# Linear attention and sparse FFN on one core: query products with the running sums as float32 instead of three fp32r passes, query pairs in four buffers, and another order on VectorE

## The chip, the cores and the metric

One core of a Trainium2 chip runs the whole program. The metric is the device time of one execution in microseconds (us). Engines: TensorE (PE; PEld is its weight load), VectorE (DVE), ScalarE (ACT), GpSimd (POOL) and SyncE (SP, which only issues transfers here).

## The reference

Input x has 2 batches x 1024 rows x 512 columns, float32. Weights have the shapes below.

```
xn  = layernorm(x)
q   = xn @ Wq.T   16 heads of 128;   k, v = xn @ Wk.T, xn @ Wv.T   4 heads of 128
q,k = rope(q), rope(k);   qf = elu(q) + 1;   kf = elu(k) + 1
for each row s:  state += kf_s (x) v_s;   z += kf_s
                 out_s = (qf_s . state) / (qf_s . z + 1e-6)
x   = x + layernorm(out @ Wo.T)
h   = silu(xn2 @ Wgate) * (xn2 @ Wup)        xn2 = layernorm(x), 512 -> 2048
h   = the two largest by magnitude of each four kept, the others 0
x   = x + layernorm(h @ Wdown)
```

Four query heads share one key and value head.

## The kernel before, in words

**Number formats.** To keep float32 precision at the fp32r matmul rate most operands are split: hi is the value rounded to fp32r, lo is the value minus hi. A product is then three passes, hi x hi, lo x hi, hi x lo (`three`, lines 453 to 456; `project`, 458 to 463, does it for four contraction blocks, twelve passes). ScalarE writes hi, GpSimd or VectorE writes lo (line 1148 on GpSimd, `split`, `query_low`, `key_low`).

**Units and slots.** The attention has 8 units (batch x key head) of 8 slots; a slot is 128 rows for the four query heads of the unit. The recurrence is done blockwise. For a block, the scores (keys x queries, line 564, bank psS) are masked causally into Sf (line 974). The result is Sf times the values (line 542), plus the queries times the running sums of the blocks before (lines 545 to 547), not in a unit's first slot. The values have two more columns, ones and zeros, so that a product of 130 columns also gives the denominator. The running sums (key rows x value rows) are accumulated in bank psSt over the unit (line 552). ScalarE copies them to Sth (line 776), VectorE takes the low half Stl (line 968). Then VectorE forms the quotient (lines 980, 983, 986) into Tn; four transposes (line 585) bring it to psS; Ah (ScalarE, line 792) and Al (VectorE, line 1006) are its halves, and one slot later the output product with Oh and Ol (line 578) is added into Y (line 1002).

**The order.** It is written out by hand for each engine: `slot_a(s)` for 65 + 1 ticks of the attention, `slot_f(n)` for the FFN, in one list TICKS (line 36). In slot s TensorE does: the products and sums of block m = s - 1; every fourth slot the transposes of the values; the scores of block s; the output product of block s - 2; the transposes of the quotient of block s - 1; every fourth slot the transposes of the keys; one query projection, `queries(s + 7)`; in some slots also the projection of keys or values (`k_slot`, `v_slot`, lines 54 to 59) and the transposes of normalised input rows (`turn`, slots IN_1, MID_0).

**Queries** come in pairs of heads (j = i // 2), one pair every two slots. For a pair VectorE rotates (`rotate`, lines 917 to 921, and `rotate_sum`, line 926). The projection of queries is laid out so that the two halves of a head stand on different banks; four transfers (`pair_rows`, lines 394 to 402, issued on SP's queue) bring them back to whole heads in the buffer xq. ScalarE takes Exp and Relu (lines 743, 744), VectorE adds them (`query_sum`, line 931), ScalarE writes the hi half (line 750), GpSimd the lo half (line 1183). The scores of block group p wait for pool_fl, which counts those lo halves. There is one buffer xq for all pairs but pair 1.

**Keys** of group p: `swap_keys` (ScalarE), `rotate_keys` (VectorE, lines 939, 940, 944), `key_terms` (ScalarE), `key_sum` (VectorE, line 948), `key_split` (ScalarE), `key_low` (GpSimd).

**Weights** come through a ring of four staging buffers. PLAN (lines 112 to 134) gives each piece the tick in which its halves are made; SP issues the load of piece k + 4 in the tick in which piece k is split, and waits for that split.

In its odd slots VectorE does rotate and rotate_sum of a pair, in its even slots query_sum and, in slots 4p - 2, rotate_keys; then the low half of the sums, the mask, the quotient, key_sum, the addition to Y, Al, output weight splits and statistics.

Of the kernel before, what the change touches and what calls it, by code (L numbers as in the profile page):

```python
# [13 lines left out]
P = 128  # L14
# [39 lines left out]
def k_slot(p):  # L54
    return 4 * p - 3 if p > 1 else -1


def v_slot(p):
    return 4 * p - 2 if p > 1 else 0
# [8 lines left out]
IN_1 = [3, 4, 7, 8, 11, 12, 15, 16]  # L68
MID_0 = [39, 40, 43, 44, 47, 48, 51, 52]
# [42 lines left out]
def weight_plan():  # L112
    plan = [(("k", 0, 0), -1), (("q", 0, 0), -1), (("q", 0, 1), -1), (("q", 0, 2), -1), (("v", 0, 0), -1),
            (("q", 0, 3), -1)] + [(("o", 0, h), -1) for h in range(4)]
    for u in range(1, UNITS + 1):
        base = 8 * (u - 1)
        more = u < UNITS
        if more:
            plan += [(("q", u, 0), (base - 2) if u > 1 else -1), (("q", u, 1), (base - 1) if u > 1 else -1), (("q", u, 2), base)]
        else:  # L120
            plan += [(("g", 0, 0), base - 1), (("g", 0, 1), base)]
        if u > 1:
            plan += [(("o", u - 1, h), base + 1) for h in range(4)]
        if more:
            plan += [(("q", u, 3), base + 2), (("k", u, 0), base + 3), (("v", u, 0), base + 4)]
# [41 lines left out]
def build(nc, x, wq, wk, wv, wo, wg, wu, wd, cos_t, sin_t, causal, eye, x1, out):  # L167
    with ExitStack() as ctx:
# [7 lines left out]
        with ExitStack() as early:  # L176
            KTr = early.enter_context(nc.sbuf_tensor("kt_rows", [P, 4, P], F32))
            Vr = early.enter_context(nc.sbuf_tensor("v_rows", [P, 4, VP], F32))
        D0h, D2h = sb("d_hi0", [P, W], F32R), sb("d_hi2", [P, VP * 4], F32R)
        Xh = sb("x_hi", [P, 4, KT, W], F32R)  # L180
# [11 lines left out]
        Dk = sb("d_lo0", [P, W], F32R)  # L192
        Dv = sb("d_lo2", [P, W], F32R)
        Uh = sb("u_hi", [P, W], F32R)
        Ul = sb("u_lo", [P, W], F32R)
        Ah = sb("a_hi", [P, 4, P], F32R)
        Al = sb("a_lo", [P, 4, P], F32R)
        Sth = sb("st_hi", [P, VP], F32R)
        Stl = sb("st_lo", [P, VP], F32R)
# [3 lines left out]
        scr = sb("scratch", [P, 16, W])  # L203
# [14 lines left out]
        M1, M2, xq = scr[:, 0:2, :], scr[:, 2:4, :], scr[:, 4:6, :]  # L218
        E = M2
        cosb = scr[:, 6:8, :]  # L220
        sinb = scr[:, 8:10, :]
        rotk, xk, Ek, Sf, zero, Tn = [scr[:, i, :] for i in range(10, 16)]
# [3 lines left out]
        def pair_of(j):  # L226
            if j == 1:
                return psOD, Y[:, 0:2, :], Y[:, 2:4, :], scr[:, 13:15, :]
            return psQ, M1, M2, xq
# [10 lines left out]
        hid = scr[:, 0:4, :]  # L240
        ab = scr[:, 4:8, :]
        sg = scr[:, 8, :]
        Wmax = [scr[:, 9, :], ab[:, 1, :]]
        msk = scr[:, 10:13, :].rearrange("p a t -> p (a t)").bitcast(BF16).rearrange("p (a t) -> p a t", a=6)
# [64 lines left out]
        act_sth, act_ah = sem("act_sth"), sem("act_ah")  # L309
        dve_q, dve_x, dve_f = sem("dve_q"), sem("dve_x"), sem("dve_f")  # L310
        dve_k1, dve_k2, dve_kx, dve_kf = sem("dve_k1"), sem("dve_k2"), sem("dve_kx"), sem("dve_kf")
        dve_stl, dve_s = sem("dve_stl"), sem("dve_s")
# [40 lines left out]
        def _(sp):  # L353
# [937 lines left out]
```

## Time and profile before

| what | value |
|---|---|
| time of the runs, median of 3 | 1279.67 us (1279.66 to 1280.18) |
| profiled execution, own time | 1280.5 us |
| its span | 1278.4 us |
| mean granted TensorE clock | 0.99 |
| TensorE, VectorE, GpSimd, ScalarE busy | 96%, 63%, 39%, 38% |
| attention slots 1 to 64 in the span | about 61 to 739 us, the FFN behind it |

How to read it: the span is from the first to the last instruction of the profiled execution; 2.1 us lie around it. A matmul's printed duration is modelled and includes the way through the array, so consecutive matmuls overlap; the distance between two starts tells what one costs. "idle before" is time without any work in flight on the engine, and behind the arrow stands what ended it. The granted clock is a share of 2.4 GHz: 1.00 is 2.4 GHz, 0.50 is 1.2 GHz.

### The profile page before, as it was taken

The page shows a single profiled execution, that of the slowest core. Times are in us where ns is not written, and L with a number is a line of the kernel's source. Part 1 is how long each engine was busy: PE and PEld are TensorE (multiplying, and loading weights), DVE is VectorE, ACT ScalarE, POOL GpSimd, SP SyncE. Part 2 cuts the span into 40 slices and gives each one's busy share as a digit, 9 for nine tenths or more (in the row PEclk, how much of TensorE's full clock was granted, in tenths as well). Part 3 has the DMA queues.
Part 4 walks back from the last instruction along what each step waited for, and adds up shares of the span by engine and source line. Part 5 has one row for each costly group of instructions (what it writes and reads, how often), then busy time and mean ns, then how long its engine had stood idle before and what let it go on. Part 6 is the DMA issues. An engine that isn't in the chain of part 4 may idle for free.

```text
span 1278.4 us, 16486 instructions
## 1 busy us (share of the span) xinstructions
PE 1232.3 (96%) x6271; PEld 1037.8 (81%) x6271; DVE 807.9 (63%) x1354; ACT 484.6 (38%) x802; POOL 498.8 (39%) x444
## 2 busy tenths in 40 slices
PE   8889999999999999999998999999999999999996
PEld 7678888788788887887886887888888878888884
DVE  8666666655766666667565655666656755555568
ACT  4433444433444434344434333333333333333322
POOL 6333342323254523334223444344435653333414
PEclk9899999999999999999998999999999999999998
DMA  5421322221323323212212321221213321111103
GB/s 185 107 67 54 86 58 51 68 57 37 96 83 107 91 58 83 62 46 84 50 34 75 107 91 58 67 67 58 58 50 99 98 75 50 43 57 42 50 1 115
DMA packets 50350, 90.33 MB, mean 71 GB/s; under 512 B 6496, under 2 KB 6752, under 8 KB 50272
## 3 DMA queue, kind: packets, MB, share of 16 engines
q1 hardware_dynamic: 50272, 89.29, 24.7%
q8 instruction: 50, 0.82, 0.3%
q14 instruction: 28, 0.23, 0.1%
HBM read 64.09 MB, written 8.39 MB: 57 GB/s over the span
## 4 chain that ended last, share of the span: by engine, by line
PE 81%; DVE 12%; ACT 2%; issue 2%; DMA 2%; SPq 1%; POOL 1%; DVEq 0%
PE bank_q L456 8%; PE bank_q L454 8%; PE bank_q L455 8%; PE bank_od L454 4%; PE bank_od L455 4%; PE bank_od L456 4%; PE bank_t L454 4%; PE bank_t L455 4%; PE bank_t L456 4%; PE bank_od L542 4%; PE bank_y L454 4%; PE bank_y L456 4%; PE bank_y L455 4%; PE bank_s L456 3%; PE bank_s L455 3%; PE bank_s L454 3%
## 5 line engine op out<-in xcount | busy, mean ns | idle before, releaser
L1148 POOL TENSOR_TENSOR big_lo<-scratch,big_hi 128x1024 fp32r<-128x1024 f32 (+1 forms) x64 | 152.2, 2388 | 346.5 <-ACT big_hi L824 214.1
L1148 POOL TENSOR_TENSOR w_lo<-stage,w_hi 128x512 fp32r<-128x512 f32 x96 | 137.1, 1436 | 148.0 <-ACT w_hi L708 147.1
L454 PE MATMUL bank_q<-x_hi,w_hi 128*128 128x512 f32 x440 | 177.7, 404 | 0.0
L456 PE MATMUL bank_q<-x_lo,w_hi 128*128 128x512 f32 x440 | 172.7, 392 | 0.0
L455 PE MATMUL bank_q<-x_hi,w_lo 128*128 128x512 f32 x440 | 171.9, 391 | 0.0
L815 ACT ACTIVATE scratch<-scratch 128x512 f32<-128x512 f32 x64 | 40.4, 632 | 207.1 <-DVE scratch L1069 207.1
L1085 DVE TENSOR_TENSOR y_acc<-bank_od,y_acc 128x512 f32<-128x512 f32 x44 | 30.2, 687 | 118.6 <-PE bank_od L456 118.6
L454 PE MATMUL bank_y<-wout_hi,a_hi 128*128 128x512 f32 x256 | 101.6, 397 | 1.6 <-POOL wout_lo L1148 1.2
L792 ACT CAST a_hi<-bank_s 128x512 fp32r<-128x512 f32 x64 | 37.5, 587 | 165.6 <-PE bank_s L585 165.6
L456 PE MATMUL bank_y<-wout_lo,a_hi 128*128 128x512 f32 x256 | 100.3, 392 | 0.0
L455 PE MATMUL bank_y<-wout_hi,a_lo 128*128 128x512 f32 x256 | 99.6, 389 | 0.0
L542 PE MATMUL bank_od<-v_rows,scratch 128*128 128x130 f32 x488 | 98.2, 291 | 0.0
L456 PEld LDWEIGHTS bank_q<-x_lo,w_hi 128*128 128x128 f32 x440 | 83.0, 189 | 18.3
L455 PEld LDWEIGHTS bank_q<-x_hi,w_lo 128*128 128x128 f32 x440 | 83.3, 189 | 15.9
L454 PEld LDWEIGHTS bank_q<-x_hi,w_hi 128*128 128x128 f32 x440 | 83.1, 189 | 15.4
L1148 POOL TENSOR_TENSOR wout_lo<-stage,wout_hi 128x512 fp32r<-128x512 f32 x28 | 44.4, 1600 | 91.4 <-ACT wout_hi L708 91.4
L542 PEld LDWEIGHTS bank_od<-v_rows,scratch 128*128 128x128 f32 x488 | 75.8, 191 | 3.8
L454 PE MATMUL bank_t<-x_hi,w_hi 128*128 128x512 f32 x192 | 77.2, 402 | 0.9 <-ACT kt_rows L728 0.7
L455 PE MATMUL bank_t<-x_hi,w_lo 128*128 128x512 f32 x192 | 76.5, 398 | 0.0
L456 PE MATMUL bank_t<-x_lo,w_hi 128*128 128x512 f32 x192 | 76.2, 397 | 0.0
L824 ACT CAST big_hi<-scratch 128x512 fp32r<-128x512 f32 x64 | 39.2, 622 | 86.5 <-DVE scratch L1041 76.1
L545 PE MATMUL bank_od<-st_hi,big_hi 128*128 128x130 f32 x212 | 65.2, 308 | 0.0
(238 smaller groups left out, 3146.9 us busy)
## 6 DMA issues: line engine op xcount, KB each, us to landing
scratch<-scratch SPq DMA_DIRECT2D x124, 128.0 KB, 2.4
x_rows<-x SPq DMA_DIRECT2D x56, 256.0 KB, 3.0
stage<-wq SPq DMA_DIRECT2D x32, 256.0 KB, 2.7
stage<-wo SPq DMA_DIRECT2D x32, 256.0 KB, 2.6
stage<-wg SPq DMA_DIRECT2D x32, 256.0 KB, 2.7
stage<-wu SPq DMA_DIRECT2D x32, 256.0 KB, 2.8
stage<-wd SPq DMA_DIRECT2D x32, 256.0 KB, 2.7
x<-x_rows SPq DMA_DIRECT2D x16, 256.0 KB, 2.5
```

Of the source, the lines that this page charges most:

```text
L454: pe.matmul(ps, whi, xhi, start=first, stop=False, skip_group_check=True)
L455: pe.matmul(ps, wlo, xhi, start=False, stop=False, skip_group_check=True)
L456: return pe.matmul(ps, whi, xlo, start=False, stop=last, skip_group_check=True)
L542: ins = pe.matmul(o, Sf[:, h * P:(h + 1) * P], Vr[:, c, :], start=True, stop=first, skip_group_check=True)
L545: pe.matmul(o, qh, Sth[:, :], start=False, stop=False, skip_group_check=True)
L792: copy(Ah[:, :, :].rearrange("p h t -> p (h t)"), psS[:, :]).then_inc(act_ah, 1)
L815: act.activation(ab[:, i, :], hid[:, i, :], ACT.Abs).then_inc(act_ab, 1)
L824: copy(big_h[:, d % 2, i, :], hid[:, i, :]).then_inc(act_hh, 1)
L1085: dve.tensor_tensor(Y[:, t, :], down_bank(y), Y[:, t, :], ALU.add).then_inc(dve_yf, 1)
L1148: return pool.tensor_tensor(dst, full, hi.bitcast(F32), ALU.subtract)
```

## The change

It has these parts:

- The product of queries and running sums is one float32 matmul per head, on rows of queries kept in Q and on one float32 copy St of the sums. Sth, Stl and line 968 go; who waited for them waits for ScalarE's copy.
- Whole heads of pairs are kept in four buffers of Q (two groups) instead of one; `pair_rows` waits for the split of three pairs before and for the products that read the buffer last.
- TensorE projects `queries(s + 6)` in slot s, not s + 7. Keys of group p are projected in slot 4p - 4 (before 4p - 3), values in 4p - 3 (before 4p - 2), and keys(1) in slot 0 instead of ahead of it. Rotation of a pair is one slot later (even slots), query_sum too (odd slots); pair_rows(2) moves behind four weight loads on SP's queue.
- On VectorE the quotient stands ahead of the mask, rotate_sum behind the mask, rotate_keys behind that, key_sum behind Al.
- Some rows' transposes and weight splits have other ticks; the scratch tiles are laid out anew (hidden gets a tile of its own, which shares memory with Q).

```diff
 def k_slot(p):
-    return 4 * p - 3 if p > 1 else -1
+    return 4 * p - 4
 def v_slot(p):
-    return 4 * p - 2 if p > 1 else 0
+    return 4 * p - 3
-IN_1 = [3, 4, 7, 8, 11, 12, 15, 16]
-MID_0 = [39, 40, 43, 44, 47, 48, 51, 52]
+IN_1 = [3, 6, 7, 10, 11, 14, 15, 18]
+MID_0 = [39, 42, 43, 46, 47, 50, 51, 54]
 # weight_plan
-            plan += [(("q", u, 0), (base - 2) if u > 1 else -1), (("q", u, 1), (base - 1) if u > 1 else -1), (("q", u, 2), base)]
+            plan += [(("q", u, 0), (base - 1) if u > 1 else -1), (("q", u, 1), base if u > 1 else -1)]
-            plan += [(("q", u, 3), base + 2), (("k", u, 0), base + 3), (("v", u, 0), base + 4)]
+            plan += [(("q", u, 2), base + 2), (("k", u, 0), base + 2), (("v", u, 0), base + 4), (("q", u, 3), base + 4)]
 # sync, pair_rows
-                if j > 1:
-                    g.wait_ge(pool_fl, pair_before(j) + 1)
+                if j > 3:
+                    g.wait_ge(pool_fl, j - 3)
+                    g.wait_ge(pe_pv, 4 * (j // 2 - 1))
-            pair_rows(2)
-                if kind == "a" and i % 2 and i <= 57:
-                    pair_rows((i + 5) // 2)
+                if kind == "a" and i % 2 == 0 and i <= 58:
+                    pair_rows((i + 4) // 2)
 # tensor
                     if not first:
-                        g.wait_ge(dve_stl, 7 * u + ms)
+                        g.wait_ge(act_st, 7 * u + ms)
                         if not first:
-                            pe.matmul(o, qh, Sth[:, :], start=False, stop=False, skip_group_check=True)
-                            pe.matmul(o, qh, Stl[:, :], start=False, stop=False, skip_group_check=True)
-                            ins = pe.matmul(o, ql, Sth[:, :], start=False, stop=True, skip_group_check=True)
+                            ins = pe.matmul(o, Q[:, (2 * p + h // 2) % 4, h % 2, t], St[:, :], start=False, stop=True,
+                                            skip_group_check=True)
-                if s + 7 < SLOTS:
-                    queries(s + 7)
+                if s + 6 < SLOTS:
+                    queries(s + 6)
-            keys(1)
 # scalar
-                        g.wait_ge(pe_pv, m)
+                        g.wait_ge(pe_pv, m + 1)
-                        copy(Sth[:, :], psSt[:, 0:VP]).then_inc(act_sth, 1)
+                        copy(St[:, :], psSt[:, 0:VP]).then_inc(act_st, 1)
-                if s % 2 == 0 and s and s + 4 < 2 * STEPS * 2:
-                    query_split((s + 4) // 2)
+                if s % 2 and s + 3 < 2 * STEPS * 2:
+                    query_split((s + 3) // 2)
-                if s % 2 and s + 5 < 2 * STEPS * 2:
-                    query_terms((s + 5) // 2)
+                if s % 2 == 0 and s + 4 < 2 * STEPS * 2:
+                    query_terms((s + 4) // 2)
 # vector, slot_a: the new order
+                if s % 2 == 0 and s + 4 < 2 * STEPS * 2:
+                    rotate((s + 4) // 2)
+                if s % 2 and s + 3 < 2 * STEPS * 2:
+                    query_sum((s + 3) // 2)
...
+                if 0 <= s < SLOTS:
...
+                if s % 2 == 0 and s + 4 < 2 * STEPS * 2:
+                    rotate_sum((s + 4) // 2)
                 for p in range(1, STEPS):
                     if s == k_slot(p) + 1:
-                        key_sum(p)
+                        rotate_keys(p)
+                if s % 4:
+                    for job in before:
+                        split_x(job)
...
+                for p in range(1, STEPS):
+                    if s == k_slot(p) + 1:
+                        key_sum(p)
 # gpsimd
-                if s % 2 == 0 and s + 4 < 2 * STEPS * 2:
-                    query_low((s + 4) // 2)
+                if s % 2 and s + 3 < 2 * STEPS * 2:
+                    query_low((s + 3) // 2)
```

In the new order of VectorE the quotient of block s - 1 stands behind rotate or query_sum and ahead of the mask of block s.

## Rows read from the trace of the kernel before

**Rows 1.** The page: busy us of each engine, share of the span, instructions.

```profile
PE 1232.3 (96%) x6271; PEld 1037.8 (81%) x6271; DVE 807.9 (63%) x1354; ACT 484.6 (38%) x802; POOL 498.8 (39%) x444
```

**Rows 2.** The page, chain that ended last: shares of the span by engine.

```profile
PE 81%; DVE 12%; ACT 2%; issue 2%; DMA 2%; SPq 1%; POOL 1%; DVEq 0%
```

**Rows 3.** List of waits, TensorE, whole span: us in total, times, longest.

```profile
PE bank_s L585 <- DVE scratch L986: 19.9, 15, 4.3
...
PE bank_y L454 <- POOL wout_lo L1148: 1.2, 1, 1.2
...
PE bank_y L454 <- DVE wout_lo L905: 0.4, 1, 0.4
```

**Rows 4.** Instructions grouped by line, TensorE, 60 to 760 us: count, busy us, mean ns.

```profile
L545 PE MATMUL bank_od<-st_hi,big_hi 128*128 128x130 f32 x212 | 65.2, 308 | 0.0
```

**Rows 5.** Timeline, TensorE, a unit's first products: start us, us, line.

```profile
61.00 1.05 PE L542 MATMUL bank_od<-v_rows,scratch 128*128 128x130 f32 x8
61.90 0.39 PE L552 MATMUL bank_st<-v_rows,kt_rows 128*128 128x130 f32 x2
62.04 0.47 PE L454 MATMUL bank_s<-big_hi,k_hi 128*128 128x512 f32 x1
```

**Rows 6.** Timeline, TensorE in a slot without a wait, and ScalarE's copy.

```profile
429.66 0.38 PE L542 MATMUL bank_od<-v_rows,scratch 128*128 128x130 f32 x2
...
432.03 0.47 PE L454 MATMUL bank_s<-big_hi,k_hi 128*128 128x512 f32 x1
...
432.81 0.40 PE L454 MATMUL bank_y<-wout_hi,a_hi 128*128 128x512 f32 x1
...
435.56 0.60 PE L585 MATMUL bank_s<-ident,scratch 128*128 128x128 f32 x4
...
438.74 0.38 PE L542 MATMUL bank_od<-v_rows,scratch 128*128 128x130 f32 x2
...
432.37 0.27 ACT L776 CAST st_hi<-bank_st 128x130 fp32r<-128x130 f32 x1 [1.93 <-PE bank_st L552]
```

**Rows 7.** Timeline, VectorE, a unit's first odd slot.

```profile
404.38 1.23 DVE L917 TENSOR_TENSOR scratch<-bank_q,scratch 128x1024 f32<-128x1024 f32 x1 [1.07 <-PE bank_q L456]
...
406.84 1.23 DVE L926 TENSOR_TENSOR scratch<-scratch 128x1024 f32<-128x1024 f32 x1
...
409.18 0.69 DVE L986 TENSOR_TENSOR scratch<-bank_od,small 128x512 f32<-128x512 f32 x1
```

**Rows 8.** Timeline, TensorE, the slot behind it: a wait at the transposes.

```profile
421.12 0.39 PE L454 MATMUL bank_y<-wout_hi,a_hi 128*128 128x512 f32 x1
...
423.69 0.66 PE L585 MATMUL bank_s<-ident,scratch 128*128 128x128 f32 x4 [1.73 <-DVE scratch L986]
```

**Rows 9.** Timeline, ScalarE behind the transfers, and VectorE's query_sum beside GpSimd's work.

```profile
412.36 1.06 ACT L743 ACTIVATE scratch<-scratch 128x1024 f32<-128x1024 f32 x1 [0.44 <-DMA scratch<-scratch]
...
330.03 2.30 DVE L931 SCALAR_TENSOR_TENSOR scratch<-scratch 128x1024 f32<-128x1024 f32 x1
```

**Rows 10.** Timeline, GpSimd in that stretch.

```profile
329.91 3.58 POOL L1148 TENSOR_TENSOR wout_lo<-stage,wout_hi 128x512 fp32r<-128x512 f32 x2 [12.13 <-ACT wout_hi L708]
```

**Rows 11.** Timeline, before and in slot 0, TensorE and SP's queue.

```profile
48.40 0.50 PE L454 MATMUL bank_t<-x_hi,w_hi 128*128 128x512 f32 x1 [0.68 <-ACT kt_rows L728]
...
52.04 0.47 PE L454 MATMUL bank_s<-big_hi,k_hi 128*128 128x512 f32 x1 [0.62 <-POOL big_lo L1148]
...
55.69 1.07 SPq L363 DMA_DIRECT2D stage<-wq  x2
```

**Rows 12.** Three stretches: us, busy time of each engine, then PEclk, DMA share, GB/s.

```profile
68.30:71.70 3.40, 3.40 (x10) 2.65 (x9) 1.48 (x3) 0.56 (x2) 1.00 (x3) 0.50 0.85 245
404.00:440.00 36.00, 33.25 (x186) 28.16 (x184) 25.26 (x39) 15.44 (x25) 17.71 (x16) 1.00 0.37 103
686.20:692.80 6.60, 5.25 (x15) 4.29 (x16) 3.90 (x9) 2.71 (x5) 4.67 (x5) 0.50 0.19 49
```

**Rows 13.** Timeline, TensorE, slot 58.

```profile
687.55 0.69 PE L585 MATMUL bank_s<-ident,scratch 128*128 128x128 f32 x2 [2.19 <-DVE scratch L986]
```

More of the change, by code:

```diff
@@ L216, in build @@
         den, share = small[:, 44:48], small[:, 48:52]
-        M1, M2, xq = scr[:, 0:2, :], scr[:, 2:4, :], scr[:, 4:6, :]
+        M1, M2 = scr[:, 0:2, :], scr[:, 2:4, :]
         E = M2
-        cosb = scr[:, 6:8, :]
-        sinb = scr[:, 8:10, :]
-        rotk, xk, Ek, Sf, zero, Tn = [scr[:, i, :] for i in range(10, 16)]
+        cosb = scr[:, 4:6, :]
+        sinb = scr[:, 6:8, :]
+        rotk, xk, Ek, Sf, Tn = [scr[:, i, :] for i in range(8, 13)]
         vT = rotk
@@ L227, in pair_of @@
             if j == 1:
-                return psOD, Y[:, 0:2, :], Y[:, 2:4, :], scr[:, 13:15, :]
-            return psQ, M1, M2, xq
+                return psOD, Y[:, 0:2, :], Y[:, 2:4, :], Q[:, 1, :, :]
+            return psQ, M1, M2, Q[:, j % 4, :, :]
         def pair_landed(gate, j):
@@ L238, in pair_before @@
             return 0 if j == 2 else j - 1
[L240 to L244, printed above, removed]
+        ab = scr[:, 0:4, :]
+        sg = scr[:, 4, :]
+        Wmax = [scr[:, 5, :], ab[:, 1, :]]
+        msk = scr[:, 6:9, :].rearrange("p a t -> p (a t)").bitcast(BF16).rearrange("p (a t) -> p a t", a=6)
         c01, c23, pw, qw, rr, m2 = [msk[:, i, :] for i in range(6)]
@@ L953, in slot_a @@
                 before = at(tick - 1, lambda j: turn_tick(*j), [j for j in TURNS if j in LATER])
-                if s % 2 and s + 5 < 2 * STEPS * 2:
-                    rotate((s + 5) // 2)
-                    rotate_sum((s + 5) // 2)
-                if s % 2 == 0 and s and s + 4 < 2 * STEPS * 2:
-                    query_sum((s + 4) // 2)
-                for p in range(1, STEPS):
-                    if s == k_slot(p) + 1:
-                        rotate_keys(p)
-                if s % 4:
-                    for job in before:
-                        split_x(job)
-                if 0 <= m < SLOTS and m % 8 < 7:
-                    i = m // 8 * 7 + m % 8
-                    g.wait_ge(act_sth, i + 1)
-                    dve.tensor_tensor(Stl[:, :], psSt[:, 0:VP], Sth[:, :].bitcast(F32),
-                                      ALU.subtract).then_inc(dve_stl, 1)
-                if 0 <= s < SLOTS:
-                    g.wait_ge(mask_ld, 16)
-                    g.wait_ge(pe_s, s + 1)
-                    g.wait_ge(pe_pv, s)
-                    dve.tensor_tensor(Sf.rearrange("p (h t) -> p h t", h=4),
-                                      psS[:, :].rearrange("p (h t) -> p h t", h=4),
-                                      mask[:, :].rearrange("p (o t) -> p o t", o=1).to_broadcast([P, 4, P]),
-                                      ALU.mult).then_inc(dve_s, 1)
+                if s % 2 == 0 and s + 4 < 2 * STEPS * 2:
+                    rotate((s + 4) // 2)
+                if s % 2 and s + 3 < 2 * STEPS * 2:
+                    query_sum((s + 3) // 2)
                 if 0 <= m < SLOTS:
@@ L988, in slot_a @@
                                       ALU.mult).then_inc(dve_a, 1)
+                if 0 <= s < SLOTS:
+                    g.wait_ge(mask_ld, 16)
+                    g.wait_ge(pe_s, s + 1)
+                    g.wait_ge(pe_pv, s)
+                    dve.tensor_tensor(Sf.rearrange("p (h t) -> p h t", h=4),
+                                      psS[:, :].rearrange("p (h t) -> p h t", h=4),
+                                      mask[:, :].rearrange("p (o t) -> p o t", o=1).to_broadcast([P, 4, P]),
+                                      ALU.mult).then_inc(dve_s, 1)
+                if s % 2 == 0 and s + 4 < 2 * STEPS * 2:
+                    rotate_sum((s + 4) // 2)
                 for p in range(1, STEPS):
                     if s == k_slot(p) + 1:
-                        key_sum(p)
+                        rotate_keys(p)
+                if s % 4:
+                    for job in before:
+                        split_x(job)
                 if 0 <= m2 < SLOTS:
@@ L1011, in slot_a @@
                         split_x(job)
-                if s == 0:
-                    query_sum(2)
                 for k in pieces_at(tick, "o"):
@@ L1134, in _ @@
             query_sum(1)
-            rotate(2)
-            rotate_sum(2)
             for kind, i in TICKS:
```

33 lines of the change are left out of this document (13 added, 20 removed).

## The prediction

> **What bounds the kernel now.** I began with the page's busy shares [rows 1]: TensorE is busy 96% of the span and VectorE 63%. The page's chain of waits gives TensorE 81% of what ended last and VectorE 12% [rows 2]. So time is won by shortening TensorE's own stream, or by removing its waits. The list of waits [rows 3] says how much the waits are: 19.9 us in 15 for line 986, the quotient on VectorE that the four transposes of line 585 read, and 1.2 + 0.4 us for output weights. Everything else there is small. All of these lie between 61 and 731 us, in the attention's 65 slots.
>
> The profiled execution took 1280.5 us (span 1278.4), the median of the runs shown is 1279.67. I add my terms to 1280.5 and take 0.8 us off at the end.
>
> **Part 1: fewer passes in the query products.** Per head, line 542 stays, and lines 545 to 547 (three fp32r products of 130 columns) become one float32 product, in 7 of a unit's 8 slots. That is 56 slots; line 545 has 212 = 4 x 53 records on bank_od [rows 4], and three slots near the end use bank_q. What a float32 product of just this shape costs is shown by the first slot of a unit, where line 542 runs alone: 8 records for 4 products, then 2 records of line 552, and the scores begin at 62.04 after a start at 61.00 [rows 5]. A float32 product is two records, and ten records take 1.03 us. From the first to the ninth record is 0.90 us, 0.112 us each. In an ordinary slot the same stretch goes from 429.66 to 432.03 [rows 6]: 2.37 us for 8 + 12 + 2 = 22 records, also near 0.11 each. After the change it has 8 + 8 + 2 = 18 records: 1.03 + 8 x 0.112 = 1.93 us. That is 0.45 us less in a slot, 56 x 0.45 = **25.0 us less**, all on TensorE's path. Its operands are others than line 542's (query rows as weights, the sums as columns), but type and shape are the same, so I take this row; the ends are 0 (as long as the three passes it replaces) and 27 us (a record at 1.03 / 10 below what I took, in all of them).
>
> The trace shows two records' time for a float32 product. The Trainium skill, in "FP8 and Floating Point Precision", section "TensorE Precision Notes", says that true FP32 makes four passes through the array, which speaks against the swap of three passes for one product. What it would do here is rival D.
>
> **Part 2: work that leaves or moves.** Line 968 (the low half of the sums, 0.28 us on VectorE) goes, and TensorE then needs only ScalarE's copy. The copy began at 432.37, the next slot's products at 438.74 [rows 6], so nothing is gained there but VectorE's time. The new waits of the row transfers (the products' count, and the split of three pairs before) were fulfilled by work of the slot before or of the same slot's beginning: nothing. Memory is laid out anew without another wait in the FFN.
>
> **Part 3: the quotient is earlier.** Before, an odd slot ran rotate, rotate_sum, low half, mask, quotient. In a unit's first odd slot rotation begins at 404.38, and the quotient's last step comes only at 409.18 [rows 7]. In the next slot key rotation and query_sum stood in front of it, and TensorE waited 1.73 us [rows 8]. This pair of waits recurs in each unit: 19.9 less 4.3 (slot 1) and 2.2 (slot 58) is 13.4 us in 13 waits. Behind the printed wait hides a little more: from the last group of line 454 at 421.12 to 423.69 is 2.57 us, where three passes need 0.69 (432.81 to 435.56 is twelve [rows 6]): 1.88 lost for a wait of 1.73; with the slower restart I take 0.2 us each, 13 x 0.2 = 2.6. After the change neither rotate_sum nor the key rotation stands ahead of the quotient. At a unit's first odd slot: query_sum 1.2 (2.3 when GpSimd works beside it [rows 9, 10]), the quotient's three steps 1.0, against transposes due at 1.03 + 0.78 + 2.75 = 4.6 us. I remove all of it: **16.0 us less**.
>
> **Part 4: the pair's round trip is tighter.** Despite its name "quotient first" leaves two things ahead of it: rotate in even slots, query_sum in odd ones. The trip from rotate_sum to query_sum is 4.3 us for four transfers (rotate_sum ends at 408.07, ScalarE begins at 412.36 [rows 7, 9]) and 2.0 us for Exp and Relu, 1.0 each. TensorE's slot becomes 1.93 (products) + 0.78 (scores) + 2.75 (output) + 3.18 (transposes and a projection) = 8.64 us by the starts [rows 6]. An elementwise step of 512 columns holds its engine 0.5 to 0.6 us, one of 1024 twice that [rows 7, 9]. With these, slot 8k+1 of unit k (10.5 us, with values): mask done 3.7 in, key rotation 2.5, then on ScalarE key terms 1.1, pair split 1.0, attention copy 0.5: 8.8; back on VectorE low half, key_sum and two output-weight splits 2.4, and hops of 0.2: 11.4. So VectorE reaches rotate of slot 8k+2 0.9 us late. Then rotate 2.4, quotient 1.0, mask 0.6, rotate_sum 1.3: 6.2; trip 6.3: 12.5, which is 3.9 into the next slot; query_sum 1.2 to 2.3 (GpSimd splits two weights then; beside its work query_sum took 2.30 [rows 9, 10]) and quotient 1.0 make 6.1 to 7.2. The transposes are due at 1.93 + 0.78 + 2.75 = 5.46. So a new wait of 0.6 to 1.7 us, I take 1.2, in seven units: **8.4 us more**, between 0 (VectorE not late) and 17. In the other half of a unit (8k+6, no output weights) rotate starts before TensorE's slot does, query_sum ends 3.8 in, the quotient at 4.9: no wait, 0.6 us to spare. Slots 8k and 8k+4 hold the keys' projection too, so their pairs come back in time. GpSimd finishes the output weights about 1 us before TensorE reads them; what is late next is that split.
>
> **Part 5: the start.** keys(1) is no longer before slot 0. Before, it filled 48.40 to 51.2 of the time in which TensorE waited for GpSimd's low half (the scores start at 52.04 [rows 11]). Now TensorE idles from 47.7 to 52.0, and the granted clock may fall as it did behind the 4.3 us wait (0.50, the 1.2 GHz level, for 3.4 us from 68.3 [rows 12], costing 1.7). pair_rows(2) now stands on SP's queue behind loads that wait for GpSimd's splits (issued at 55.69 [rows 11]), so it starts near 56.3: ScalarE at 60.8, done 62.8, query_sum 64.1, quotient 65.1, after which query(7) and values(1) end at 71.1, 72.8 with the clock. Before, slot 2 began at 72.1 with one projection more (2.8 us) done. **3.5 us more**, between 0 and 7.
>
> **Part 6: the end.** Slot 57 gains query(63) and values(15), so the output weights are ready for slot 58: the waits of 1.2, 0.4 and 2.2 us [rows 3, 13] go, 4.4 with their restarts. But slots 58 and 59 are now about 5.9 us, and pair 31 is rotated in slot 58: rotate_sum ends 5.0 in, trip to 11.4, query_sum and quotient to 13.7, against transposes due at 5.9 + 5.5 = 11.4: a wait of 2.3 (2.5). The clock fell there to 0.50 for 6.6 us, costing 3.3 [rows 12]; with one wait in place of three I count half of it. 4.4 - 2.5 + 1.7 = **3.6 us less**, between 0 and 6.
>
> **The sum.** -25.0 - 16.0 + 8.4 + 3.5 - 3.6 = -32.7; 1280.5 - 32.7 - 0.8 = **1247.0 us**.
>
> **The rivals.**
> A. The new waits of part 4 don't come, because VectorE is not late: -41.1, so 1238.6. For: in the wait of rows 8 VectorE was held by work that moves behind the quotient. Against: the walk above has it over by 0.6 even at its best.
> B. The waits of part 4 are twice as long or bring falls of the clock (1.7 us each in seven units, 12 us): +8 to +12, 1255 to 1259. For: a wait of 4.3 us was followed by one. Against: waits up to 1.7 us were not; the clock was 1.00 from 404 to 440, which holds two of them [rows 12].
> C. **It ends slower: the pair's return becomes the bound.** Place: query_sum in every odd slot, ahead of the quotient. Let the trip be 2.5 us longer than 6.3 (transfers queued behind weight loads on SP, ScalarE held by key_terms). Then 8k+3 waits 3.7, 8k+7 1.9, 8k+1 and 8k+5 about 1.3 together: 6.9 x 7 = 48 in place of 8.4, 1287. It decides against the change from about 2.2 us on. Against: the trip was 4.3 and 2.0 us here, and SP's blocks end before the transfers are due.
> D. The float32 product takes four passes of 0.112 us where three stood: +0.112 x 4 x 56 = +25 in place of -25, 1297. Against: a product of this type and shape took two records of 0.112 [rows 5]. The Trainium skill's page named in part 1 has this rule.
> E. The change does not do what it says: if VectorE held TensorE back in every slot, the saved passes would turn into waits and only parts 3 to 6 count, 1272. Against: 96% on TensorE.
>
> **How the numbers follow.** Forecast 0.50, A 0.18, B 0.20, C 0.05, D 0.02, E 0.05. The range takes in A and B with the bounds of parts 5 and 6 (3.5 us on either side each) and what the walks of parts 4 to 6 miss: 1233 to 1266. C, D and E are outside, 0.12, and a little of A beyond its bounds, 0.06. Faster by over 0.2% are the forecast, A, B, E and a thin end of C; 0.2% (2.6 us) is about what a measurement of this kernel can tell from no change. Faster 0.92, same 0.02, slower 0.06.
>
> **What would show it.** Right: line 546 and 547 gone and one product with two records per head; from the first product to the scores 1.93 us; TensorE's waits for line 986 gone from slots 8k+1 and 8k+2 and standing in 8k+3 at about 1.2 us, one near slot 59; idle of 4 us before slot 0's scores. Wrong: a slot's product stretch above 2.1 us (part 1), waits in 8k+7 or 8k+1 (part 4), waits on output weights, or a granted clock of 0.5 within the units.

## The result and the profile after

The changed kernel takes **1300.18 us** (median of 4 runs, 1296.48 to 1303.86) where the kernel before takes 1279.66 beside it: ratio 1.0163, 95% interval [1.0137, 1.0189]. It is slower by 1.6%. The forecast was 1247.0, within 1233 to 1266, with 0.92 on faster: **wrong in sign**. The profiled execution took 1296.48 us (span 1294.7), 16.0 more than the one of before.

The page of the changed kernel, busy shares, and the chain that ended last (they answer to [rows 1] and [rows 2]):

```profile
PE 1217.1 (94%) x6047; PEld 1022.3 (79%) x6047; DVE 808.6 (62%) x1298; ACT 482.7 (37%) x802; POOL 487.6 (38%) x444
...
PE 69%; DVE 19%; ACT 4%; issue 3%; DMA 2%; SPq 1%; POOL 1%; DVEq 0%; ACTq 0%
```

TensorE has 224 instructions less, as it should (four a slot in 56 slots), yet its share of the chain fell from 81% to 69%; VectorE's rose from 12% to 19%, ScalarE's from 2% to 4%. The time went into waits. The list of TensorE's waits (us in total, times, longest), to set beside [rows 3]:

```profile
PE bank_s L581 <- DVE scratch L963: 26.9, 13, 5.0
PE bank_t L480 <- DVE x_lo L888: 22.8, 6, 4.3
...
PE bank_s L452 <- POOL big_lo L1130: 4.3, 1, 4.3
```

The 19.9 us for the quotient are gone. In their place stand 26.9 us for the mask (line 963: the transposes write the scores' bank, which the mask must have read), and 22.8 us, in only six waits, for x_lo, the low half of transposed rows of x. The prediction does not name that tile. (Both lists also hold one wait of 6.5 us for x_lo on bank_s, before slot 0; it is the same in both kernels.)

**The product is as cheap as forecast.** TensorE's timeline in slot 36, from the first product to the work behind it (it answers to [rows 6]):

```profile
446.01 0.39 PE L539 MATMUL bank_od<-v_rows,scratch 128*128 128x130 f32 x2
446.23 0.39 PE L542 MATMUL bank_od<-st_rows,q_rows 128*128 128x130 f32 x2
...
447.80 0.39 PE L548 MATMUL bank_st<-v_rows,kt_rows 128*128 128x130 f32 x2
448.02 0.60 PE L501 MATMUL bank_t<-ident,scratch 128*128 128x128 f32 x4
```

From 446.01 to 448.02 are 18 records in 2.01 us, 0.112 each, and from the products to the sums' product 1.79 for 16. Slot 11, shown below, goes from its first product at 170.89 to its scores at 172.82: 1.93 us, the forecast. A plain slot (one without a projection of keys or values, a turn of x rows or a wait, such as slot 38), start to start, takes 8.66 us; the forecast was 8.64, and the kernel before had 9.09.

**Where the time came from.** From the first product of slot 1 to that of slot 64 it took 664.8 us before and 681.6 now: +16.8, all of the difference between the profiled executions. Six slots carry more than that: 7, 11, 15, 43, 47 and 51 take 12.60, 16.06, 12.57, 16.05, 12.57 and 16.21 us, 28.8 more than the same six before. Those are the slots 4p - 1 in which x rows are turned (IN_1, MID_0). The timeline of all engines at one of them, slot 11:

```profile
170.46 0.60 PE L480 MATMUL bank_t<-ident,x_rows 128*128 128x128 f32 x4
...
170.89 0.39 PE L539 MATMUL bank_od<-v_rows,scratch 128*128 128x130 f32 x2
...
172.45 1.06 ACT L736 ACTIVATE scratch<-q_rows 128x1024 f32<-128x1024 f32 x1 [3.24 <-DMA q_rows<-scratch]
...
172.82 0.48 PE L452 MATMUL bank_s<-big_hi,k_hi 128*128 128x512 f32 x1
...
173.42 1.04 ACT L737 ACTIVATE q_rows<-q_rows 128x1024 f32<-128x1024 f32 x1
174.37 1.12 ACT L701 CAST w_hi<-stage 128x512 fp32r<-128x512 f32 x2
174.49 1.23 DVE L921 SCALAR_TENSOR_TENSOR q_rows<-scratch,q_rows 128x1024 f32<-128x1024 f32 x1 [5.06 <-ACT q_rows L737]
...
175.39 0.57 ACT L676 CAST x_hi<-bank_t 128x512 fp32r<-128x512 f32 x1
...
176.65 0.68 DVE L963 TENSOR_TENSOR scratch<-bank_s,mask 128x512 f32<-128x512 f32 x1
177.24 0.68 DVE L888 TENSOR_TENSOR x_lo<-bank_t,x_hi 128x512 fp32r<-128x512 f32 x1
...
178.07 0.87 PE L480 MATMUL bank_t<-ident,x_rows 128*128 128x128 f32 x3 [4.31 <-DVE x_lo L888]
```

One row of x is turned at the end of slot 4p - 2, the next in the middle of slot 4p - 1, **ahead of the output product, into the same bank**. Between the two the bank must be read twice. But ScalarE stands idle for 3.24 us in query_terms until the pair lands, then does Exp, Relu and two weight splits before x_hi (175.39); VectorE has query_sum, the quotient and the mask ahead of x_lo (177.24). TensorE stands for 4.31 us, and its output product behind it. Before, the turns were in slots 4p - 1 and 4p (transposes into bank_t at 127.94 in slot 7, 144.08 in slot 8, 171.96 in slot 11), never less than 16 us apart.

The clock follows. Windows of the changed kernel (us, busy time of PE, PEld, DVE, ACT, POOL, then PEclk, DMA share, GB/s), behind the waits of slots 7, 11 and 43:

```profile
130.60:136.00 5.40, 5.40 (x28) 4.54 (x29) 1.68 (x3) 2.64 (x4) 2.82 (x2) 1.00 0.01 3
...
176.60:183.30 6.70, 5.23 (x15) 4.29 (x16) 1.32 (x3) 1.58 (x3) 5.06 (x4) 0.50 0.36 117
...
528.20:534.90 6.70, 5.38 (x15) 4.44 (x16) 1.18 (x2) 1.53 (x2) 4.92 (x4) 0.50 0.34 120
```

Behind slot 7's wait of 3.30 us the clock stayed at 1.00; behind the two of 4.3 it was 0.50, the 1.2 GHz level, for some 6.7 us, and so it was behind slot 51's. That goes with slots 11, 43 and 51 being 3.5 us longer than the other three: 1.0 by the wait, and half of the 5.2 to 5.7 busy us at half clock.

### The profile page after: what moved, and what is told of

It is laid out like the page before. It is cut to its first block, busy times and chain, and to the rows that moved or that the text cites. A ratio compares the mean times of both kernels' runs of the same rounds, so it can differ in the third digit from the quotient of the medians.

```text
span 1294.7 us, 15921 instructions
## 1 busy us (share of the span) xinstructions
PE 1217.1 (94%) x6047; PEld 1022.3 (79%) x6047; DVE 808.6 (62%) x1298; ACT 482.7 (37%) x802; POOL 487.6 (38%) x444
## 4 chain that ended last, share of the span: by engine, by line
PE 69%; DVE 19%; ACT 4%; issue 3%; DMA 2%; SPq 1%; POOL 1%; DVEq 0%; ACTq 0%
PE bank_q L454 7%; PE bank_q L452 7%; PE bank_q L453 7%; PE bank_od L452 4%; PE bank_od L453 4%; PE bank_od L454 4%; PE bank_t L454 3%; PE bank_t L453 3%; PE bank_t L452 3%; PE bank_od L539 3%; PE bank_s L452 3%; PE bank_s L453 3%; PE bank_s L454 3%; PE bank_y L452 3%; PE bank_y L453 3%
## 5 line engine op out<-in xcount | busy, mean ns | idle before, releaser
L1130 POOL TENSOR_TENSOR big_lo<-hidden,big_hi 128x512 fp32r<-128x512 f32 x32 | 73.6, 2320 | 214.5 <-ACT big_hi L814 214.5
L805 ACT ACTIVATE scratch<-hidden 128x512 f32<-128x512 f32 x64 | 40.5, 634 | 206.9 <-DVE hidden L1053 206.9
L921 DVE SCALAR_TENSOR_TENSOR q_rows<-scratch,q_rows 128x1024 f32<-128x1024 f32 x31 | 38.0, 1226 | 126.2 <-ACT q_rows L737 126.2
L1130 POOL TENSOR_TENSOR big_lo<-q_rows,big_hi 128x1024 fp32r<-128x1024 f32 x32 | 76.5, 2392 | 98.8 <-ACT big_hi L743 98.7
L453 PE MATMUL bank_y<-wout_hi,a_lo 128*128 128x512 f32 x256 | 102.4, 400 | 0.0
L539 PE MATMUL bank_od<-v_rows,scratch 128*128 128x130 f32 x488 | 91.2, 276 | 0.0
L542 PE MATMUL bank_od<-st_rows,q_rows 128*128 128x130 f32 x424 | 82.7, 277 | 0.0
```

Of the source, the lines that this page charges most:

```text
L453: pe.matmul(ps, wlo, xhi, start=False, stop=False, skip_group_check=True)
L539: ins = pe.matmul(o, Sf[:, h * P:(h + 1) * P], Vr[:, c, :], start=True, stop=first, skip_group_check=True)
L542: ins = pe.matmul(o, Q[:, (2 * p + h // 2) % 4, h % 2, t], St[:, :], start=False, stop=True, skip_group_check=True)
L805: act.activation(ab[:, i, :], hid[:, i, :], ACT.Abs).then_inc(act_ab, 1)
L921: dve.scalar_tensor_tensor(whole, grown, 1.0, whole, ALU.min, ALU.add).then_inc(dve_f, 1)
L1130: return pool.tensor_tensor(dst, full, hi.bitcast(F32), ALU.subtract)
```

## The experiments

Each run stood beside the kernel before on the same chip; "after" is the changed kernel. Differences between two kernels are of their medians.

**1. The rows of x first.**

```diff
 # scalar: in slot 4p - 2 ahead of query_terms, not behind it in 4p - 1
+                if s % 4 == 2:
+                    for job in at(tick, lambda j: turn_tick(*j), [j for j in TURNS if j in LATER]):
+                        split_x(job)
 # vector: in slot 4p - 1 ahead of query_sum, not behind the mask
+                if s % 4 == 3:
+                    for job in before:
+                        split_x(job)
```

> The changed kernel, but the two halves of the input rows that TensorE turns at the end of slots 4p - 2 (slots 6, 10, 14, 18 and 42, 46, 50, 54) are made earlier: ScalarE makes x_hi ahead of query_terms in the same slot, VectorE makes x_lo ahead of query_sum in the next. Theory 1 (the saving of the products is real, and the six waits of TensorE for x_lo with the falls of the clock behind them ate it): the 22.8 us of waits for line 888's x_lo go, with their restarts (about 1 us) and the half-clock stretches behind the three of 4.3 us (3 x 6.8 us at half rate, 10 us); 1300 - 30, so 1264 to 1274, faster than the kernel before. Theory 2 (the waits are cover, VectorE and the pair's trip bound these slots anyway): the wait moves to line 963 in the same slots, and no more than 8 us are won, 1292 or above. Theory 3 (the clock falls because of the float32 products, not because of waits): the waits go but the stretches of half clock stay, 1276 to 1280.

Measured: 1267.93 us (1267.13 to 1269.18), ratio 0.9907 [0.9891, 0.9924]; 32 us below after (27 between the profiled executions). Four of the six slots are 9.1 us, slots 43 and 51 are 9.8; in sum they are 30.1 less. The waits for x_lo in bank_t are gone; those for the mask stay:

```profile
PE bank_s L581 <- DVE scratch L966: 28.4, 17, 5.1
```

So the turn of x alone turns a gain into a loss: with two moved calls the change is faster than before. Theory 3 fell too: the float32 products are all there, yet in slots 2 to 56 the stretches of half clock fell from 23.9 us in all to 6.8, and in run 5 there is none.

**2. Three passes again, on the changed kernel.** Sth and Stl in place of St; nothing else differs.

```diff
-                            ins = pe.matmul(o, Q[:, (2 * p + h // 2) % 4, h % 2, t], St[:, :], start=False, stop=True,
-                                            skip_group_check=True)
+                            pe.matmul(o, qh, Sth[:, :], start=False, stop=False, skip_group_check=True)
+                            pe.matmul(o, qh, Stl[:, :], start=False, stop=False, skip_group_check=True)
+                            ins = pe.matmul(o, ql, Sth[:, :], start=False, stop=True, skip_group_check=True)
```

> The changed kernel with its order and buffers, but the product with the running sums again in three fp32r passes with Sth and Stl. Theory 1: 4 x 56 passes more at 0.112 us, 25 us slower than the changed kernel less what its waits absorb (of the 27 us of waits for line 963 perhaps 5), 1318 to 1326. Rival D (a float32 product costs four passes): about 25 us faster, 1275. Theory 3: the clock falls less often, so less than 15 us slower, 1310 or below.

Measured: 1312.57 us (1311.21 to 1314.26), ratio 1.0259 [1.0243, 1.0274]; 12.4 above after. The sign is as expected, the size too small. The list of waits says where the rest went:

```profile
PE bank_s L584 <- DVE scratch L966: 18.9, 12, 4.1
PE bank_t L481 <- DVE x_lo L891: 18.7, 6, 4.1
```

The two are 12.1 us shorter in sum than in after, 8.0 of it at the mask: a TensorE that is slower by 25 us waits 12 us less. Run 10 tests that reading.

**3. The mask ahead of the quotient on VectorE.** The block of line 963 is moved up, nothing else.

> The changed kernel with the mask ahead of the quotient on VectorE again, all else as changed. The transposes write the bank that the mask reads, so they wait for both. Theory 1: the order of the two is worth nothing, within 4 us of the changed kernel (1296 to 1304). Rival (quotient first saves a wait for the products' end or brings the transposes forward, as the prediction had it): 7 to 15 us slower.

Measured: 1312.45 us (1310.01 to 1313.5), ratio 1.0254 [1.0239, 1.027]; 12.3 above after. The expectation of no difference fell, its rival was right. Both waits grew; line 964 is now the quotient, which comes last of the two. VectorE's own list has a new wait, that of the mask (line 952) for the scores:

```profile
PE bank_s L581 <- DVE scratch L964: 29.4, 15, 4.3
PE bank_t L480 <- DVE x_lo L888: 24.1, 6, 4.3
...
DVE scratch L952 <- PE bank_s L454: 26.9, 32, 3.0
```

The quotient's 1 us fills the time in which the scores are still being made; with the mask first VectorE waits for them, and what follows is later. The two waits of TensorE grew by 3.8 us only, and output weights add 2.5; about 5 us of the rest go with stretches of half clock, 10 us more of them in the attention. The change's "quotient first" is worth keeping.

**4. As 1, with query_sum behind the mask in odd slots.**

> As e1_x_early, and query_sum stands behind the mask in odd slots, so that the quotient and the mask are first there. Theory 1: besides what e1 wins, the waits for line 963 in slots 4p - 1 go (some ten of 0.9 to 1.6 us and the one of 5 us near slot 59), with falls of the clock; 10 to 18 us below e1, 1248 to 1262. Rival (the pair's low half is then late for the scores of slot 4p): the wait goes to the scores' first pass for big_lo, and e4 is within 4 us of e1 or above it.

Measured: 1271.19 us (1270.12 to 1273.07), ratio 0.9936 [0.9921, 0.9951]; 3.3 above run 1. The waits for the mask fell from 28.4 to 18.1, but output weights (4.0 in 7), issue (4.1 in 3) and the copy of the sums (2.2) took their place. Query_sum in front of the mask does hold it (slots 19 and 27 fall from 10.1 and 10.2 us to 8.7 and 8.6), but the later place costs as much elsewhere (slot 60: 9.15 to 12.41).

**5. As 1, with the keys' Exp and Relu behind the attention copy on ScalarE.** In after, key_terms waits for the rotated keys ahead of the split of queries and the copy Ah.

```diff
 # scalar, slot 4p - 3
-                    if s == k_slot(p) + 1:
-                        key_terms(p)
...
+                for p in range(1, STEPS):
+                    if s == k_slot(p) + 1:
+                        key_terms(p)
```

> As e1_x_early, and in slots 4p - 3 ScalarE does key_terms behind the copy of the transposed quotient instead of ahead of it. Theory 1 (what is left of the loss is a chain in each unit's first odd slot: key_terms holds ScalarE until VectorE's key rotation, so the pair's split, the quotient's copy and the output weights come late, VectorE and GpSimd then split beside each other at half rate, and VectorE reaches the rotation of slot 8k + 2 some 3 us after its queries are there): the waits of 1.4 to 2.2 us in slots 8k + 2 go and those in 8k + 3 shrink, about 3 us in each of seven units, and one or two falls of the clock: 16 to 24 us below e1, 1244 to 1252. Rival (the pair's trip alone bounds 8k + 2 and 8k + 3, wherever VectorE's slot ends): within 4 us of e1, 1264 to 1272.

Measured: 1242.8 us (1242.14 to 1243.5), ratio 0.9705 [0.9689, 0.9722]; 25 below run 1, a little more than expected. The waits for the mask fall from 28.4 us in 17 to:

```profile
PE bank_s L581 <- DVE scratch L967: 8.2, 5, 3.7
```

Side by side, first the changed kernel's timelines of slots 33 and 34 (products from 413.84 and 424.33), ScalarE, VectorE, GpSimd and TensorE one after the other:

```profile
418.75 0.63 ACT L725 ACTIVATE scratch<-scratch 128x512 f32<-128x512 f32 x1 [3.21 <-DVE scratch L934]
...
420.75 0.57 ACT L785 CAST a_hi<-bank_s 128x512 fp32r<-128x512 f32 x1
...
421.97 1.92 DVE L938 SCALAR_TENSOR_TENSOR scratch<-scratch 128x512 f32<-128x512 f32 x1
423.81 3.45 DVE L895 TENSOR_TENSOR wout_lo<-stage,wout_hi 128x512 fp32r<-128x512 f32 x2
...
428.00 1.22 DVE L907 TENSOR_TENSOR scratch<-bank_q,scratch 128x1024 f32<-128x1024 f32 x1
...
431.35 0.68 DVE L963 TENSOR_TENSOR scratch<-bank_s,mask 128x512 f32<-128x512 f32 x1
...
420.93 2.41 POOL L1130 TENSOR_TENSOR big_lo<-q_rows,big_hi 128x1024 fp32r<-128x1024 f32 x1 [2.08 <-ACT big_hi L743]
423.67 3.04 POOL L1130 TENSOR_TENSOR wout_lo<-stage,wout_hi 128x512 fp32r<-128x512 f32 x2 [0.33 <-ACT wout_hi L701]
...
432.18 0.79 PE L581 MATMUL bank_s<-ident,scratch 128*128 128x128 f32 x4 [2.24 <-DVE scratch L963]
```

Then the fifth kernel's, the same two slots (from 389.90 and 400.36):

```profile
395.12 0.59 ACT L780 CAST a_hi<-bank_s 128x512 fp32r<-128x512 f32 x1 [2.54 <-PE bank_s L581]
395.60 0.64 ACT L725 ACTIVATE scratch<-scratch 128x512 f32<-128x512 f32 x1
...
396.79 1.05 DVE L939 SCALAR_TENSOR_TENSOR scratch<-scratch 128x512 f32<-128x512 f32 x1 [0.36 <-ACT scratch L726]
398.00 1.29 DVE L896 TENSOR_TENSOR wout_lo<-stage,wout_hi 128x512 fp32r<-128x512 f32 x2 [0.16 <-ACT wout_hi L701]
...
400.04 1.22 DVE L908 TENSOR_TENSOR scratch<-bank_q,scratch 128x1024 f32<-128x1024 f32 x1
...
394.88 2.41 POOL L1131 TENSOR_TENSOR big_lo<-q_rows,big_hi 128x1024 fp32r<-128x1024 f32 x1
...
405.84 0.60 PE L581 MATMUL bank_s<-ident,scratch 128*128 128x128 f32 x4
```

In after the attention copy comes 6.9 us into the slot, in the fifth kernel 5.2. The later copy pushes VectorE's key_sum and its two weight splits beside GpSimd's two pieces of work, where they take 1.92 and 3.45 us and not 1.05 and 1.29. So rotation of the pair starts 3.7 us behind the next slot's beginning, in the fifth kernel 0.3 ahead of it, and the quotient and mask stand behind rotation.

**6. As 5, with the start as before**: keys(1), rotate(2) and rotate_sum(2) ahead of slot 0, values(1) in slot 0, pair_rows(2) ahead of the four loads.

> As e5_attention_copy_first, and the start as in the kernel before: keys(1) and rotate(2), rotate_sum(2) ahead of slot 0, values(1) in slot 0, pair_rows(2) ahead of the four weight loads. By the traces, the products of slot 2 begin at 73.8 us in the changed kernel and at 72.1 in the one before, which has one projection of 2.8 us more behind it. Theory 1 (the start cost 4.5 us, by an idle TensorE before slot 0 and a trip that began behind SP's waits, and two falls of the clock): 4 to 7 us below e5. Rival (the time lost at the start was only moved, slots 1 to 4 wait for the pairs anyway): within 2 us of e5.

Measured: 1239.0 us (1237.36 to 1240.07), ratio 0.9676 [0.9661, 0.9691]; 3.8 below run 5, just short of the 4 to 7 expected and clear of the rival's 2. TensorE's timeline shows what is left of the start, in slot 1:

```profile
63.71 0.63 PE L582 MATMUL bank_s<-ident,scratch 128*128 128x128 f32 x4 [3.50 <-DVE scratch L969]
```

**7. After, with only VectorE's half of edit 1.**

> The changed kernel with only VectorE's part of e1: x_lo ahead of query_sum in slots 4p - 1, while ScalarE still makes x_hi behind the pair's transfers, Exp and Relu. Theory 1 (x_hi itself comes late, because ScalarE stands in query_terms until the transfers land): of the 31.7 us that e1 won only about 1.2 us per turn is won, 5 to 10 us in all, 1290 to 1296. Rival (VectorE's own order was the cause, x_lo behind query_sum, quotient and mask): nearly all is won, 1266 to 1272.

Measured: 1286.99 us (1284.8 to 1287.59), ratio 1.0049 [1.0033, 1.0065]; 13 below after, somewhat more than expected and far from the rival's 30. The six waits for x_lo are 9.0 us in place of 22.8, while those for the mask grew from 26.9 to 32.3. Both engines' orders hold the bank, and ScalarE's, standing ahead of VectorE's, is what is left.

**8. The kernel before, with only VectorE's new order**: quotient, mask, rotate_sum, rotate_keys, low half; three passes, one buffer, all slots as before.

> The kernel before with nothing of the change but the order on VectorE: quotient, mask, then rotate_sum, rotate_keys, then the low half of the sums. Three fp32r passes, one pair buffer, seven slots ahead. By part 3 of the prediction the 13 waits of the transposes go, 10 to 16 us faster than the kernel before, 1264 to 1270. Rival (the order gives back what it takes, since rotate_sum, and so query_sum and ScalarE's queue, come later by as much as the quotient comes sooner): within 3 us of the kernel before or slower, 1277 or above.

Measured: 1266.75 us (1264.85 to 1268.53), ratio 0.9894 [0.9877, 0.9911]; 13.5 below before. The list of waits:

```profile
PE bank_y L454 <- POOL wout_lo L1149: 5.2, 6, 1.2
PE bank_s L585 <- DVE scratch L973: 4.5, 3, 2.4
...
PE bank_y L454 <- DVE wout_lo L905: 2.0, 1, 2.0
```

The 19.9 us of [rows 3] are 4.5; the output weights are late next, as part 4 named it. This edit of a few lines gives the time that it promised without the rest of the change, but not where it was promised: in slots 2 to 57, where part 3's 13 waits stand, it gave 7.0 us, and the rest at the two ends, 3.5 in slot 1 and 3.2 from slot 58 on.

**9. As 6, with VectorE's order changed at both ends**: query_sum(2) behind slot 1's mask, and the last rotate_sum ahead of slot 58's quotient.

> Edit: the sixth kernel, with the query sum of pair 2 put behind slot 1's mask on VectorE, and, in slot 58, the sum of the last pair's rotated keys put directly behind the rotation, ahead of the quotient. What is left in the sixth kernel are two waits of TensorE for its scores: 3.5 us in slot 1 (VectorE stands in the query sum of pair 2, ahead of the mask) and 2.83 us in slot 59 (the low half of the last pair's rows comes late), each with a stretch of half clock of 3.4 to 6.8 us behind it. Theory 1 (both waits are VectorE's order alone): the wait in slot 1 falls below 1 us and the one in slot 59 by about 2 us, and with the half clock behind them, 1.7 us a stretch, the kernel comes 5 to 9 us below the sixth, at 1230 to 1234 us. Theory 2 (the waits only move one slot on, to slot 2 and slot 60, since VectorE has the same work there): within 2 us of the sixth kernel, 1237 to 1241 us.

Measured: **1234.5 us** (1233.66 to 1235.28), ratio 0.9641 [0.9625, 0.9657]; 4.5 below run 6, half a microsecond short of the expected band. TensorE's timeline in slot 1 and slot 59:

```profile
61.79 0.63 PE L582 MATMUL bank_s<-ident,scratch 128*128 128x128 f32 x4 [0.96 <-DVE scratch L971]
...
654.60 0.63 PE L582 MATMUL bank_s<-ident,scratch 128*128 128x128 f32 x4 [2.30 <-DVE scratch L971]
```

Slot 1's wait went as theory 1 had it. Slot 59 got only 0.5 us shorter (8.87 to 8.34), where 2 were expected. It is the fastest kernel here, 3.6% below before.

**10. As 5, with three passes.** Run 2's edit where the waits are gone.

> Edit: the fifth kernel with the product of queries and running sum in three float32r passes (high and low parts of the running sum in the two buffers of before) in place of the one float32 product, all else as it is. The same edit on the changed kernel cost 12.4 us where the count gives 25 (four records of 0.11 us in each of 56 slots). Theory 1 (the other half was taken up by the waits of the x rows' turn, which aren't there in the fifth kernel): the full price shows, 24 to 28 us above the fifth kernel, 1266 to 1271 us. Theory 2 (the running sum's extra two records hide beside something else in every slot, waits or not): again about half, 1254 to 1258 us. Theory 3 (the float32 product is the dearer one): below 1242 us.

Measured: 1263.82 us (1262.23 to 1265.61), ratio 0.9873 [0.9858, 0.9887]; 21.0 above run 5. That is 2 us below the band of theory 1 and 6 above that of theory 2. Its product stretch, TensorE's timeline:

```profile
442.76 0.38 PE L540 MATMUL bank_od<-v_rows,scratch 128*128 128x130 f32 x2
442.90 0.31 PE L544 MATMUL bank_od<-st_hi,big_hi 128*128 128x130 f32 x1
...
445.13 0.47 PE L453 MATMUL bank_s<-big_hi,k_hi 128*128 128x512 f32 x1
```

2.37 us again, as in [rows 6]. Plain slots are 9.10 us in place of 8.64. The slots where run 5 is longer than a plain slot by a wait (19, 35 and 39, also 11, 43, 51, 59 and 60) grew by less or not at all: 9.10 after 9.16 in slot 19, 9.09 after 9.33 in slot 35. Slot by slot, that is the 4.5 us which are missing of 55 x 0.45.

## Why the prediction was wrong

Term by term, in us:

| term | forecast | measured | from |
|---|---|---|---|
| 1, products | -25.0 | about -25; 21.0 as seen from run 5 | slots of 8.66 after 9.09; run 10 |
| 2, work that moves | 0 | +32 | run 1 against after |
| 3, quotient earlier | -16.0 | -13.5, but -7.0 in slots 2 to 57 | run 8 |
| 4, pair's trip | +8.4 | about +25, 21.8 of it in slots 2 to 57 | run 5 against run 1 |
| 5, start | +3.5 | +4.5 | slot 2 begins at 73.80, was 72.08; one projection (2.8) less done |
| 6, end | -3.6 | about -0.2 | slots 57 to 63: 55.05 after 57.97, less 6 x 0.45 that term 1 holds |
| sum | -32.7 | about +23 | measured +20.5 |

The terms don't add exactly, as run 2 shows, and those of runs 5 and 8 reach into the ends, which terms 5 and 6 hold too. The sum is a check of size, no more.

**Part 2 is the step that failed**: it put the work that moves at nothing without a reason for the x rows. "Memory is laid out anew without another wait in the FFN" is all that the prediction says to the change's last bullet, and the two lines IN_1 and MID_0 were never costed. They move the turn at the end of slot 4p to the end of slot 4p + 2, while the next stays in slot 4p + 3. Since one is at its slot's end and the other ahead of its slot's output product, a distance of over 16 us became 3.3 us (in slot 11 from 170.46 to 173.76, where the wait of 4.31 begins), with two engines' reads of the bank in between. What the runs showed in place of 0 is +32 us: 22.8 us of waits in six slots, with 6.8 us of half clock behind three of them. The walk of part 4 had all it took to see that: ScalarE's landing of the pair, query_sum, quotient and mask, in the order of the code. Runs 1 and 7 show both the place and that both engines' orders count.

**Part 4 was the right mechanism and the wrong size**, by a factor of three, and partly the wrong slot. The walk has VectorE reach rotate 11.4 us into slot 8k + 1 (0.9 late); measured are 14.2 (428.00 - 413.84, 3.7 late). The walk took key_sum and the two weight splits at 2.4 us with the low half; key_sum and splits alone took 5.4 beside GpSimd (1.92 + 3.45). For query_sum the prediction had that effect from [rows 9, 10], and used it nowhere else. Statistics of y (0.9) were missing too. Then the wait comes in 8k + 3, where it was forecast, only in part (1.57 us in slot 19 and 1.36 in 27), and mostly one slot earlier, where quotient and mask stand behind rotation: 2.24 us in slot 34. Rival C named the place "query_sum in every odd slot"; run 4, which takes it out of there and gains nothing, speaks against it as the bound.

**The clock.** Rival B had falls of the clock behind longer waits; they came, but by waits that it did not foresee. The text that "waits up to 1.7 us were not" followed by one holds no bound from above: behind the 2.24 us wait in slot 34 the clock was 0.50 for 3.4 us. Nor does the length of a wait settle it: three other waits of 2.24 us (slots 10, 42 and 50) and the three of 3.30 were followed by no fall.

**Part 1 was right**, in records (two a product), in length and in where it counts. Rival D is refuted by both run 2 and run 10: three passes are dearer by 12.4 and 21.0 us. The Trainium skill ("FP8 and Floating Point Precision", section "TensorE Precision Notes") gives four passes for true FP32, and the rows don't contradict it: a group of 512 fp32r columns takes 0.23 us here, so 130 columns are 0.058 by length alone, and four of them 0.23 by this estimate, about what a float32 product takes (0.22). What rival D had wrong was the price of a pass: the 0.112 us of an fp32r pass of 130 columns is about twice that length and was multiplied by four. That the rest of such a pass is its weight load (190 ns in the profile) is a reading of mine, not tried.

**Parts 3, 5 and 6.** Part 5 was right within 1 us, with the 4.3 us for big_lo ahead of slot 0's scores as it named them. Part 3's account of what makes the quotient late is shown by run 8, whose waits for the quotient fall from 19.9 to 4.5 us; that the total comes within 3 us of the 16.0 is partly luck, since 6.7 us of it lie at the ends, which part 3 had left out. In slots 2 to 57 TensorE waits 13.5 us before and 7.3 in run 8 (5.2 of it for output weights, which come late next), but 1.5 in run 5. Which of the change's other parts takes the waits for output weights away was not tried. Run 3 adds what part 3 left out: the transposes wait for the mask as well, since they write its bank, so that "quotient first" works because it costs the mask nothing. Part 6 lies within its bounds, but by another sum: slot 59 waits 5.0 us (2.3 were forecast) and slot 58 still 1.5.

**The first reading** was too short: "Everything else there is small" passes over three waits of 6.5, 2.8 and 2.7 us outside the attention. They stand unchanged in every run, so nothing hung on it.

The chance of slower, 0.06, was put on single mechanisms priced from walks, with nothing for parts of the diff that had no walk at all.

## What to carry to other kernels

When a change moves work between slots, list for each bank and buffer who writes it, who must read it and who writes it next, for every moved line of the diff, also those that look like bookkeeping; a write that comes nearer to the one before is a new wait. In an engine's handwritten order, put short work that another engine stands for ahead of work that waits for a transfer. A saved pass shows at its full price only where its engine doesn't wait: here the same edit was worth 12 us in one order and 21 in another.

## What the runs showed of the hardware

**VectorE and GpSimd hold each other up.** Groups by line, VectorE, first the changed kernel:

```profile
L895 DVE TENSOR_TENSOR wout_lo<-stage,wout_hi 128x512 fp32r<-128x512 f32 x24 | 30.8, 1308 | 1.4 <-ACT wout_hi L701 1.4
L938 DVE SCALAR_TENSOR_TENSOR scratch<-scratch 128x512 f32<-128x512 f32 x16 | 29.4, 1838 | 1.2 <-ACT scratch L726 1.2
```

and the fifth kernel:

```profile
L931 DVE SCALAR_TENSOR_TENSOR scratch<-scratch,small 128x512 f32<-128x512 f32 x16 | 34.8, 2175 | 0.0
L896 DVE TENSOR_TENSOR wout_lo<-stage,wout_hi 128x512 fp32r<-128x512 f32 x24 | 15.7, 682 | 3.6 <-ACT wout_hi L701 3.6
L939 DVE SCALAR_TENSOR_TENSOR scratch<-scratch 128x512 f32<-128x512 f32 x16 | 12.9, 805 | 2.8 <-ACT scratch L726 2.5
```

The same instruction takes 682 or 1308 ns in the mean, by what GpSimd does beside it; in the fifth kernel the loss has moved to the key rotation (2175 ns), where nobody stands for it. In the changed kernel key_sum began at 421.97 and ended at 423.89, 0.55 us behind GpSimd's split (420.93 + 2.41): it did little until GpSimd was done. All 15 key_sums that began during such a split took 1.90 to 1.93 us and ended 0.55 us behind it; the one that began alone took 0.69. The order of the starts decides: query_sum (1.23 us), when it began first, lost nothing, and the 22 weight splits that GpSimd began during it took 1.81 us in place of 1.29. An operation with one of its two inputs in a PSUM bank is not held: Al (line 989) took 0.69 us in all 25 cases beside GpSimd's split. The Trainium skill's "SBUF — State Buffer", section "Who interferes with whom", has it as an exclusive lock on a shared pair of ports, which a VectorE instruction with two SBUF inputs needs beside a GpSimd instruction that reads SBUF; by the page's summary the second to issue stands until the first ends. The trace agrees. Durations of two-input VectorE work are thus no constants, and a walk should ask what GpSimd is doing at that moment.

**An fp32r pass of 130 columns costs half of one of 512** (0.11 against 0.23 us), and a float32 product of 130 columns as much as two of them, so that for products of this shape float32 beats the three-pass split (runs 2 and 10). Other lengths were not tried.
